# Group norm of layer 1 moved into the spectral transform, and the attention's weights multiplied out there

## The chip, the cores and the metric

The kernel runs on one core of a Trainium2 chip. The time is the device time of one execution in microseconds (us), and the figure of a kernel is the median of its runs. The granted clock of TensorE is a second number of each run: it has two levels, 1.2 and 2.4 GHz, shown as 0.50 and 1.00.

## The reference

The input is x of shape (4, 32, 128, 128) in float32: four batches of 32 images of 128 rows by 128 channels. Layers follow one another; each adds its result to x. Layer 0 is a graph attention and a state-space scan, layers 2 and 3 are attention, experts and a recurrence; none of them is touched. Layer 1 computes

```python
x = x + codano(gn(x))        # gn: 32 groups of 4 channels, over the 32 images of a batch
...
tokens = gn(x).reshape(128, 1, 128, 128)
tokens_norm = instance_norm(tokens)            # mean and variance of each image
k = fno_layer(tokens_norm, key_w, ..., (64, 64)); q = fno_layer(..., query_w, ...)
v = fno_layer(tokens_norm, value_w, ..., (128, 128))          # 16 heads from one channel
dprod = softmax(q . k over the 64*64 pixels)   # tokens of one batch against each other
attn = fno_layer(dprod @ v, proj_w, ...); attn = instance_norm(attn + tokens)
m = mixer(attn); out = instance_norm(m) + attn
```

where `fno_layer` is a product of low Fourier modes with weights plus a 1x1 skip path. Since a head differs from another by weights only, the products of query and key reduce to a Gram matrix of the 64x64 transforms of all tokens (skip paths) and to a few low modes (spectral weights).

## The kernel before, in words

All blocks run one after the other; between two blocks every engine meets at a barrier. Inside a block each engine has its own program, written out in order, and waits on semaphores (`wait_ge`); `Chain` makes each VectorE or GpSimd step wait for the one before it. All transfers go out on SyncE, in program order.

`group_norm` (L96) takes x one batch (2 MB) at a time into two buffers. ScalarE squares it (L130), TensorE sums columns by a matrix of ones (L140, L144), VectorE reduces to groups (L163), GpSimd takes the power -0.5 (L155) and VectorE normalises 128x4096 values twice (L176, L177) into `hg`, 8 MB in SBUF. SyncE waits for each load to land before it issues the next.

`token_spectra` (L1358) loads its tables, stores `hg` to the DRAM tensor `tokens` with one transfer (L1402), and then

- transforms rows: TensorE multiplies each image by a table of 65 columns (L1426), four images (a unit) per PSUM bank, and ScalarE copies them into `o1` (L1467), four banks in turn;
- takes statistics of every image on VectorE (L1497), has them totalled by two matmuls (L1431, L1432), and derives the instance norm's scale (L1508 to L1518), with one power on GpSimd (L1417);
- transforms columns (L1437 to L1442) into `z`, which ScalarE copies (L1474 to L1479); computes the low modes `xh` (L1448, L1450), which ScalarE scales (L1483); and sums the Gram matrix over 65 column blocks (L1457, L1458), scales it by a diagonal matmul (L1461) and stores it (L1404).

`token_attention` (L1557) loads the query and key weights and biases by 58 small transfers (L1622 to L1634), multiplies them out on VectorE into `da`, `db`, `row`, `r0` and `coef` (L1727 to L1772), meanwhile transposes the low modes on TensorE (L1667, L1668), and only then copies the transposed modes (L1776) and forms the heads' operands (L1784 on), scores, softmax and probabilities `pt`.

`attended_spectrum` (L1833) loads value and projection weights by 24 small transfers (L1871 to L1886), multiplies them into `w` on VectorE (L1923 to L1939), stores it to DRAM (`mode_weights`, L1890), and reads it back once per head, broadcast to all partitions (L1895); VectorE multiplies `xh` by it for 16 heads (L1947 to L1955) and TensorE mixes (L1981).

`graph_attention` (L181, layer 0) is not changed, but has in its prologue the group norm that the change uses: 16 chunks of eight images, each 512 KB, loaded on their own (L266), squared on ScalarE (L491), summed by a 128x32 matrix of ones in four column groups of the array, two for values and two for squares (L374), a reduction (L573), a matmul to group sums (L358), small VectorE and GpSimd steps, and two matmuls (L363, L364) that spread scale and shift over channels.

Of the kernel before, what the change touches and what calls it, by code (L numbers as in the profile page):

```python
# [13 lines left out]
f32 = mybir.dt.float32  # L14
# [6 lines left out]
P = 128  # L21
# [72 lines left out]


def group_norm(nc, src, hg, tag, G=32, eps=1e-5):  # L96

    J = C // G
    N = T * W * J
    with ExitStack() as ctx:  # L100
        s = Scope(nc, ctx, tag)
        xb = s.sb("xb", [P, 2, T * C])
        sq = s.sb("sq", [P, T * C])
        ones = s.sb("ones", [P, P])
        sums = s.sb("sums", [P, 2, G])
        var = s.sb("var", [P, G])
        rstd = s.sb("rstd", [P, G])
        half = s.sb("half", [P, G])
        ps = [s.ps(f"ps{j}") for j in range(2)]
        loaded, squared, summed, var_done, rstd_done, normed, ready = (  # L110
            s.sem(n) for n in ("loaded", "squared", "summed", "var_done", "rstd_done", "normed", "ready"))
        dch = s.sem("dch")
        block = ctx.enter_context(nc.Block())

        @block.sync
        def _(sp):
            for b in range(B):
                if b >= 2:
                    sp.wait_ge(normed, b - 1)
                sp.dma_start(xb[:, b % 2, :].rearrange("w (t c) -> w t c", t=T),  # L120
                             src[b].rearrange("t w c -> w t c")).then_inc(loaded, 16)
                sp.wait_ge(loaded, 16 * b + 16)

        @block.scalar
        def _(act):
            for b in range(B):
                act.wait_ge(loaded, 16 * b + 16)
                if b >= 1:
                    act.wait_ge(summed, b)
                act.activation(sq[:, :], xb[:, b % 2, :], ACT.Square).then_inc(squared, 1)  # L130

        @block.tensor
        def _(pe):
            pe.wait_ge(ready, 1)
            for b in range(B):
                pe.wait_ge(loaded, 16 * b + 16)
                if b >= 1:
                    pe.wait_ge(var_done, b)
                for j in range(8):
                    pe.matmul(ps[0][:, :], ones[:, :], xb[:, b % 2, 512 * j:512 * j + 512],  # L140
                              start=(j == 0), stop=(j == 7))
# [1178 lines left out]
SR = 64  # L1320
# [3076 lines left out]
```

## Time and profile before

| | us |
|---|---|
| median of 3 runs | 4502.13 (4489.3 to 4511.93) |
| the profiled execution | 4496.7 |
| its span | 4495.0 |
| TensorE matmul busy | 3571.1 (79%) |
| VectorE busy | 3190.4 (71%) |
| ScalarE busy | 2643.9 (59%) |
| GpSimd busy | 2526.4 (56%) |
| mean granted TensorE clock | 0.852 |

The durations in this text are from the profiled execution, whose own time is 1.7 us more than its span. A time such as 2518.35 is counted from the span's start. Busy shares are averages over all layers; for one block the windows and the timelines are read. In the rows PE is TensorE, PEld its weight loads, DVE VectorE, ACT ScalarE, POOL GpSimd, SP or SPq SyncE. A float32 matmul appears as two records (passes).

### The profile page before, as it was taken

The numbers are of one execution on the slowest core, as the hardware profiler recorded it, in microseconds if no ns is written. First come the engines' busy times: TensorE is split into PE (matmuls) and PEld (weight loads), VectorE is DVE, ScalarE is ACT, GpSimd is POOL, SyncE is SP. The second block draws the span as 40 slices with busy tenths as digits, with TensorE's granted clock in tenths as the row PEclk, the third lists the DMA queues.
The fourth block names the chain that finished last, engine by engine and source line by source line (L and its number), as shares of the span: only waits on it lengthen the run. The fifth ranks groups of instructions, "written<-read, shape, count | busy, mean of one in ns | idle before, by whom it ended". The sixth has DMA issues, their size and how long they took to land. (4 is left out here: it accounts for less than half of the span.)

```text
span 4495.0 us, 83074 instructions
## 1 busy us (share of the span) xinstructions
PE 3571.1 (79%) x29188; PEld 2331.2 (52%) x29188; DVE 3190.4 (71%) x6169; ACT 2643.9 (59%) x5155; POOL 2526.4 (56%) x2910
## 2 busy tenths in 40 slices
PE   7996599999999999999999676547884885658767
PEld 4764255555555555555555365315663652346636
DVE  4996388888888888888888342526994856159854
ACT  6885477778777778777787120004774627138553
POOL 4997678787787887787875210004785413012650
PEclk9998699999999999999999865676776977779678
DMA  3001000000000000000000230241222114760233
GB/s 83 25 25 48 7 4 20 20 11 20 20 20 20 16 15 20 20 20 20 11 18 23 72 85 2 81 167 57 76 62 70 52 52 115 251 167 1 62 90 108
DMA packets 376049, 231.29 MB, mean 51 GB/s; under 512 B 44288, under 2 KB 350920, under 8 KB 373576
## 3 DMA queue, kind: packets, MB, share of 16 engines
q1 hardware_dynamic: 375640, 225.98, 17.6%
q8 instruction: 239, 3.92, 0.4%
q14 instruction: 170, 1.39, 0.1%
HBM read 150.15 MB, written 75.76 MB: 50 GB/s over the span
## 5 line engine op out<-in xcount | busy, mean ns | idle before, releaser
L1222 DVE TENSOR_TENSOR_SCAN mam_hs<-mam_dA,mam_ps_b 128x1024 f32<-128x1024 f32 x512 | 1156.4, 2275 | 2.3 <-PE mam_ps_b L1027 2.1
L1041 PEld LDWEIGHTS mam_ps_h<-mam_ident,mam_hs 128*128 128x128 f32 x4096 | 460.4, 146 | 426.4 <-issue 422.6
L1027 PE MATMUL mam_ps_b<-mam_DB,mam_dtxt 32*128 32x512 f32 x2048 | 589.6, 651 | 85.6 <-DVE mam_hs L1222 82.8
L1160 ACT ACTIVATE mam_dA<-mam_dt,mam_A 128x496 f32<-128x496 f32 x1024 | 649.3, 703 | 0.7
L1168 ACT COPY mam_hTb<-mam_ps_h 128x512 f32<-128x512 f32 x768 | 424.9, 583 | 324.2 <-PE mam_ps_h L1041 320.3
L1041 PE MATMUL mam_ps_h<-mam_ident,mam_hs 128*128 128x128 f32 x4096 | 585.2, 288 | 27.7 <-ACT mam_hTb L1168 26.5
L825 POOL TENSOR_SCALAR mam_tap<-mam_xcp,mam_cw 128x512 f32<-128x512 f32 x192 | 300.7, 1566 | 18.7
L1232 DVE COPY mam_hTb<-mam_ps_h 128x512 f32<-128x512 f32 x256 | 175.9, 687 | 179.0 <-PE mam_ps_h L1041 179.0
L1053 PE MATMUL mam_ps_y<-mam_hTb,mam_WC 128*32 128x128 f32 x8192 | 281.3, 278 | 0.4 <-issue 0.4
L1053 PEld LDWEIGHTS mam_ps_y<-mam_hTb,mam_WC 128*32 128x32 f32 x8192 | 212.3, 111 | 122.6 <-issue 93.2
L1027 PEld LDWEIGHTS mam_ps_b<-mam_DB,mam_dtxt 32*128 32x128 f32 x2048 | 158.1, 186 | 221.6 <-issue 220.0
L826 POOL TENSOR_TENSOR mam_xs<-mam_xs,mam_tap 128x512 f32<-128x512 f32 x192 | 244.0, 1271 | 16.0
L855 POOL TENSOR_TENSOR mam_WC<-mam_cp,mam_m 128x128 f32<-128x128 f32 x512 | 220.4, 463 | 5.9 <-PE mam_ps_y L1053 5.7
L524 ACT ACTIVATE gat_ex<-gat_ps_s,gat_neg 128x128 f32<-128x128 f32 x512 | 154.5, 436 | 50.6 <-DVE gat_neg L607 50.6
L2227 POOL TENSOR_TENSOR l1t_rs<-l1t_va,l1t_half 128x8 f32<-128x8 f32 x64 | 108.1, 1689 | 126.0 <-DVE l1t_va L2547 125.8
L823 POOL TENSOR_SCALAR mam_xs<-mam_xcp,mam_cw 128x512 f32<-128x512 f32 x64 | 100.4, 1568 | 121.8 <-ACT mam_xcp L1113 121.4
L847 POOL TENSOR_TENSOR mam_DB<-mam_bt,mam_m 128x512 f32<-128x512 f32 x128 | 147.5, 1153 | 6.9 <-PE mam_ps_b L1027 6.5
L320 POOL TENSOR_TENSOR gat_ex<-gat_ex,gat_den 128x512 f32<-128x512 f32 x128 | 132.9, 1049 | 28.3 <-DVE gat_den L616 28.3
L966 PE MATMUL mam_ps<-mam_xs,mam_wdt 128*128 128x512 f32 x256 | 126.6, 618 | 5.3 <-issue 2.8
L831 POOL TENSOR_SCALAR mam_po<-mam_e 128x512 f32<-128x512 f32 x64 | 52.2, 816 | 137.8 <-ACT mam_e L1136 134.9
L3666 POOL MEMSET sma_half<- 128x4 f32 x1 | 0.1, 101 | 198.7 <-POOLq L81 198.7
L836 POOL TENSOR_TENSOR mam_dt<-mam_dt,mam_ln 128x512 f32<-128x512 f32 x64 | 81.7, 1277 | 47.9 <-DVE mam_ln L1260 47.9
(693 smaller groups left out, 8640.0 us busy)
## 6 DMA issues: line engine op xcount, KB each, us to landing
moe_wg<-in_L_ffn_weight SPq DMA_DIRECT2D x32, 1024.0 KB, 8.0
rnn_xr<-x SPq DMA_DIRECT2D x23, 512.0 KB, 5.4
l1y_wh<-mode_weights SPq DMA_DIRECT2D x16, 544.0 KB, 3.7
gat_hg<-in_x SPq DMA_DIRECT2D x16, 512.0 KB, 7.2
h<-gat_out SPq DMA_DIRECT2D x32, 256.0 KB, 2.3
mam_ht<-h SPq DMA_DIRECT2D x128, 64.0 KB, 2.0
mam_hr<-h SPq DMA_DIRECT2D x128, 64.0 KB, 2.0
mam_xt<-in_x SPq DMA_DIRECT2D x128, 64.0 KB, 2.0
```

What stands on the lines that cost most here:

```text
L524: last = act.activation(ex[:, i % 2, h, r, :], ps_s[h][:, r * W:(r + 1) * W], ACT.Exp, bias=neg[:, i % 2, h, r:r + 1])
L825: step(pool.tensor_scalar(tap[:, :, :], xcp[:, h, :, k:k + T], cw[:, h, k:k + 1], None, ALU.mult))
L826: step(pool.tensor_tensor(acc, acc, tap[:, :, :], ALU.add))
L847: pool.tensor_tensor(DB[:, g, :, :], bt[:, i % 2, g, :].unsqueeze(2).broadcast_to([P, S, T]), m32[:, :].unsqueeze(1).broadcast_to([P, S, T ...
L855: last = pool.tensor_tensor(WC[:, j, g, :, :], cp[:, i % 2, j, g, :].unsqueeze(2).broadcast_to([P, S4, T]), m32[:, :].unsqueeze(1).broadca ...
L1027: last = pe.matmul(ps_b[w % 2][:, n, :], steps[r, g * P:(g + 1) * P], DB[r, g, :, :].rearrange("p s t -> p (s t)"), start=True, stop=True, ...
L1041: last = pe.transpose(ps_h[n][:, q * P:(q + 1) * P], hs[:, w % 3, c:c + P], ident[:, :])
L1053: last = pe.matmul(ps_y[j * T:(j + 1) * T, g * P:(g + 1) * P], WC[:, j, g, q, :], hTb[:, gg % 2, j, q, :], start=(q == 0), stop=(q == S4 - 1),
L1160: act.activation(dA[:, h, :, n, 1:], dt[:, i % 2, h, :].rearrange("p (q t) -> p q t", q=Q)[:, :, 1:], ACT.Exp, scale=A[:, h, n:n + 1]).the ...
L1168: act.copy(hTb[:, gg % 2, j, :, :], ps_h[n][:, :].rearrange("p (q d) -> p q d", q=S4)).then_inc(hB_ready if n else hA_ready, 1)
L1222: dve.tensor_tensor_scan(hs[:, w % 3, :], dA[:, h, first:first + 2, :, :].rearrange("p q s t -> p (q s t)"), ps_b[w % 2][:, :, :].rearrang ...
L1232: dve.tensor_copy(hTb[:, gg % 2, 2 * (w % 2) + 1, :, :], ps_h[1][:, :].rearrange("p (q d) -> p q d", q=S4)).then_inc(hB_ready, 1)
```

## The change

The block `group_norm` is gone. `token_spectra` takes x itself. It loads x as 16 chunks of eight images into `hg` without waiting, sums them as graph attention's prologue does, and transforms the raw images' rows at once. ScalarE, which copies a unit's row transform out, now scales it by its channel's factor (`colsc`), for which it waits for the batch's norm (`norm_ready`); a channel's shift touches only the mode of row frequency 0, and VectorE adds it there (`constant_modes`). TensorE's order interleaves, for each batch, eight units with the four sums of the batch behind, and then the two group matmuls of that batch. VectorE makes the normalised tokens in three buffers of eight images (`normed`), from which the statistics are taken and which SyncE stores chunk by chunk (`save`).

The 58 and 24 small weight loads stand on SyncE between those stores, and the weights' products on VectorE behind the statistics. The totals of the instance norm come after the Gram matmuls on TensorE; `xh` is copied unscaled and scaled once at the end on VectorE. The two blocks behind lose these loads and products, and take the results from SBUF and DRAM. The tile `spec` is allocated after this block in place of before it.

```diff
+            for j in range(NC):
+                b, t0 = divmod(j * CH, T)
+                sp.dma_start(hg[:, j * CH:(j + 1) * CH, :], x1[b, t0:t0 + CH].rearrange("t w c -> w t c")
+                             ).then_inc(xin[j], 16)
...
+            def save(j):
+                sp.wait_ge(hn_ready, j + 1)
+                sp.dma_start(tok[j * CH:(j + 1) * CH].rearrange("n r c -> r n c"), hn[:, j % HB, :, :]
+                             ).then_inc(saved[j % HB], 16)
...
+            save(0)
...
+            for j, (name, ta, tb, tr) in enumerate((("query_w", qa, qb, qr), ("key_w", ka, kb, kr))):
+                src = wts[name][0].rearrange("h y x a -> y x h a")
+                for y in range(LKY):
+                    sp.dma_start(ta[y * L:(y + 1) * L, :, :], src[y, 1:LKX]).then_inc(w_loaded, 16)
+                    n += 1
+                save(2 + 2 * j)
+                sp.dma_start(tb[0:HF, :, :], src[0:HF, 0]).then_inc(w_loaded, 16)
+                sp.dma_start(tr[0:1, :, :], src[0:1, 0]).then_inc(w_loaded, 16)
...
+                save(3 + 2 * j)
...
+            assert n == WLOADS, (n, WLOADS)
+            for j in range(7, NC):
+                save(j)
+            sp.wait_ge(w_ready, 1)
+            sp.dma_start(wd.rearrange("h y a x -> y h a x"), mw[:, :, :, :]).then_inc(w_out, 16)
             sp.wait_ge(g_ready, 1)
             sp.dma_start(gram_d, gs[:, :]).then_inc(stored, 16)
             sp.wait_ge(stored, 16)
-            sp.wait_ge(saved, 16)
+            sp.wait_ge(w_out, 16)
+            for j in range(HB):
+                sp.wait_ge(saved[j], 16 * len(range(j, NC, HB)))
 
         @block.gpsimd
         def _(pool):
...
+            def sums(j):
+                pe.wait_ge(xin[j], 16)
+                pe.wait_ge(squared, j + 1)
+                b = j // CB
+                if j % CB == 0 and b >= 2:
+                    pe.wait_ge(red_ready, b - 1)
+                v, v2 = chunk(j), sq[:, j % 2, :]
+                for q, src in enumerate((v[:, 0:512], v[:, 512:1024], v2[:, 0:512], v2[:, 512:1024])):
+                    last = pe.matmul(ps_x[b % 2][32 * q:32 * q + 32, :], ones[:, :], src, start=(j % CB == 0),
+                                     stop=(j % CB == CB - 1), tile_position=(0, 32 * q))
+                last.then_inc(sums_done, 1)
+
+            def groups(b):
+                pe.wait_ge(red_ready, b + 1)
+                pe.matmul(ps_s[0:G, 4 * b:4 * b + 4], red[:, :], sel[:, :], start=True, stop=True).then_inc(grouped, 1)
+
+            def channels(b):
+                pe.wait_ge(wide_ready, b + 1)
+                pe.matmul(ps_s[:, 64 + 4 * b:68 + 4 * b], ext[:, :], gr[:, b, :], start=True, stop=True)
+                pe.matmul(ps_g[:, 0:2 * C], onesr[:, :], wide2[:, :, :].rearrange("p a c -> p (a c)"),
+                          start=True, stop=True).then_inc(spread, 1)
+
...
             pe.wait_ge(made, 1)
-            pe.wait_ge(summed, 1)
-            pe.matmul(ps_s[:, 0:4], su[:, :], mean_w[:, :], start=True, stop=True)
-            pe.matmul(ps_s[:, 4:8], sv[:, :], square_w[:, :], start=True, stop=True).then_inc(totalled, 1)
+            for j in range(CB):
+                sums(j)
+            pe.wait_ge(loaded, 80)
+            UB = UNITS // B
+            for b in range(B):
+                for i in range(CB):
+                    row_modes(UB * b + 2 * i)
+                    if b == 0 and i == 0:
+                        groups(0)
+                    if b < B - 1:
+                        sums(CB * (b + 1) + i)
+                    row_modes(UB * b + 2 * i + 1)
+                    if b == 0 and i == 0:
+                        channels(0)
+                if b < B - 1:
+                    groups(b + 1)
+                    channels(b + 1)
             pe.wait_ge(copied, UNITS)
...
+            pe.wait_ge(summed, 1)
+            pe.matmul(ps_s[:, 128:132], su[:, :], mean_w[:, :], start=True, stop=True)
+            pe.matmul(ps_s[:, 132:136], sv2[:, :], square_w[:, :], start=True, stop=True).then_inc(totalled, 1)
             pe.wait_ge(g_read, 1)
             pe.wait_ge(d_ready, 1)
-            pe.matmul(ps_s[:, 128:256], g0[:, :], diag[:, :], start=True, stop=True).then_inc(d_done, 1)
+            pe.matmul(ps_s[:, 256:384], g0[:, :], diag[:, :], start=True, stop=True).then_inc(d_done, 1)
 
...
+            def squares(j):
+                act.wait_ge(xin[j], 16)
+                if j >= 2:
+                    act.wait_ge(sums_done, j - 1)
+                act.activation(sq[:, j % 2, :], chunk(j), ACT.Square).then_inc(squared, 1)
+
+            def row_modes(u):
+                b = u * R // T
                 act.wait_ge(done, u + 1)
-                act.copy(o1[:, :, u * R:(u + 1) * R], ps[u % 4][:, 0:R * KA].rearrange("p (r k) -> p k r", r=R)
-                         ).then_inc(copied, 1)
+                act.wait_ge(norm_ready, b + 1)
+                act.activation(o1[:, :, u * R:(u + 1) * R], ps[u % 4][:, 0:R * KA].rearrange("p (r k) -> p k r", r=R),
+                               ACT.Identity, scale=colsc[:, b, 0:1]).then_inc(copied, 1)
+
...
+            def group_norm_of(b):
+                dve.wait_ge(sums_done, CB * (b + 1))
+                if b >= 1:
+                    dve.wait_ge(grouped, b)
+                step(dve.tensor_reduce(red[:, :], ps_x[b % 2][:, :].rearrange("p (t g j) -> p g t j", g=G, j=J), AX.XY,
+                                       ALU.add))
+                dve.sem_inc(red_ready, 1)
...
+                step.mark(dve.tensor_copy(rowsc[:, b, :, :], ps_g[:, 0:2 * C].rearrange("p (a c) -> p a c", a=2)))
+                step.join()
+                dve.sem_inc(norm_ready, 1)
+
...
+            def normed(j):
+                b, dst = j // CB, hn[:, j % HB, :, :]
+                if j >= HB:
+                    dve.wait_ge(saved[j % HB], 16 * (j // HB))
+                every = [P, CH, C]
+                step(TT(dst, hg[:, j * CH:(j + 1) * CH, :], rowsc[:, b, 0, :].unsqueeze(1).broadcast_to(every), ALU.mult))
+                step(TT(dst, dst, rowsc[:, b, 1, :].unsqueeze(1).broadcast_to(every), ALU.add))
+                dve.sem_inc(hn_ready, 1)
+                for n in range(CH):
+                    step.mark(dve.bn_stats(st[:, j * CH + n, :], hn[:, j % HB, n, :]))
+                step.join()
+
+            def constant_modes(b):
+                dve.wait_ge(copied, UNITS // B * (b + 1))
+                TS(o1[:, 0, batch(b)], o1[:, 0, batch(b)], colsc[:, b, 1:2], None, ALU.add).then_inc(k_fixed, 1)
+
+            group_norm_of(0)
+            for j in range(NC):
+                normed(j)
+                if j in (2, 5, 8):
+                    group_norm_of(j // 3 + 1)
+                if j in (5, 8, 10, 11):
+                    constant_modes((5, 8, 10, 11).index(j))
...
-        with nc.sbuf_tensor("hg1", [P, BT, C], f32) as hg:
-            group_norm(nc, x1, hg, "gn1")
-            token_spectra(nc, hg, wts["norm1_g"], wts["norm1_b"], tabs, xh, gram, tok, nrm)
...
-            dve.wait_ge(loaded, 16 * LOADS)
-            dve.wait_ge(prepared, 1)
+            dve.wait_ge(w_loaded, 16 * WLOADS)
+            dve.wait_ge(zeroed, 2)
...
+            step.mark(TT(sv[:, :, 0, 1], sv[:, :, 0, 1], rv[:, :, 1], ALU.subtract))
+            step.mark(TT(mw[:, :, 0, :], pr, vs.broadcast_to(full), ALU.mult))
...
+            dve.wait_ge(loaded, 80)
+            dve.wait_ge(totalled, 1)
+            step(dve.tensor_copy(mv[:, :], ps_s[:, 128:136].rearrange("p (a b) -> p a b", a=2)[:, :, 0]))
...
+            step.mark(TS(diag[:, :], ident[:, :], nrm[:, 0:1], None, ALU.mult))
+            step.join()
+            dve.sem_inc(nrm_ready, 1)
+            dve.sem_inc(d_ready, 1)
+            dve.wait_ge(x_read, NB)
+            step(TS(xh[:, :, :, :], xh[:, :, :, :], nrm[:, 0:1], None, ALU.mult))
+            step(dve.tensor_copy(xh[:, 0, 0, 0:1], gb[:, 1:2]))
...
-            dve.wait_ge(loaded, 16 * NL)
```

The lines that follow `dve.wait_ge(w_loaded, ...)` in the new `token_spectra` are the old ones of L1727 to L1772 and L1923 to L1939, moved; likewise the loads. Their names differ (`mw` for `w`, `sk`, `pskip`).

## Rows read from the trace of the kernel before

**Rows 1.** Windows: length; busy (count) of PE, PEld, DVE, ACT, POOL; PE clock; DMA.

```profile
2518.30:2620.60 102.30, 61.65 (x128) 26.15 (x128) 42.09 (x24) 14.47 (x4) 21.98 (x6) 0.80 0.30 82
2620.60:2680.80 60.20, 55.47 (x260) 55.47 (x261) 26.53 (x133) 12.04 (x32) 0.66 (x5) 0.50 0.51 143
2680.80:2753.40 72.60, 68.26 (x295) 56.74 (x295) 1.80 (x11) 12.65 (x25) 0.56 (x1) 0.62 0.01 1
...
2844.20:2872.90 28.70, 0.00 (x0) 0.00 (x0) 4.28 (x19) 0.00 (x0) 2.68 (x5) 0.50 0.21 39
```

**Rows 2.** Timeline of SyncE, group norm: start, us, line, transfer.

```profile
2518.35 61.40 SPq L120 DMA_DIRECT2D gn_xb<-x  x4
```

**Rows 3.** Timeline of TensorE, token spectra, key rows.

```profile
2625.33 54.87 PE L1426 MATMUL l1f_ps<-l1f_rows,hg 128*128 128x65 f32 x256 [22.42 <-DMA l1f_gb<-in_L_conv_norm_b]
2680.00 0.53 PE L1431 MATMUL l1f_ps_s<-l1f_mean_w,l1f_su 128*128 128x4 f32 x2
...
2680.82 15.55 PE L1437 MATMUL l1f_ps<-l1f_o,l1f_cols 128*65 128x512 f32 x34
...
2747.47 0.79 PE L1458 MATMUL l1f_ps_g<-l1f_zp 64*128 64x128 f32 x2
2748.62 0.80 PE L1461 MATMUL l1f_ps_s<-l1f_diag,l1f_g 128*128 128x128 f32 x2 [0.35 <-ACT l1f_g L1487]
```

**Rows 4.** Timeline of VectorE, token spectra, first and last of the chain.

```profile
2681.10 0.16 DVE L1508 COPY l1f_mv<-l1f_ps_s 128x2 f32<-128x2 f32 x1 [33.80 <-PE l1f_ps_s L1432]
...
2683.18 0.28 DVE L1518 TENSOR_SCALAR l1f_diag<-l1f_ident,nrm 128x128 f32<-128x128 f32 x1
```

**Rows 5.** Windows: graph attention's start, and the column transform L1437.

```profile
44.70:48.40 3.70, 2.77 (x6) 1.18 (x6) 0.00 (x0) 0.78 (x1) 1.26 (x1) 0.50 0.01 2
...
2684.00:2696.90 12.90, 12.90 (x36) 4.39 (x34) 0.00 (x0) 9.02 (x16) 0.00 (x0) 1.00 0.00 0
```

**Rows 6.** Graph attention's prologue: timelines of SyncE, ScalarE, TensorE; tile ps_s.

```profile
0.81 4.22 SPq L266 DMA_DIRECT2D gat_hg<-in_x  x4
...
10.17 21.00 SPq L266 DMA_DIRECT2D gat_hg<-in_x  x12
...
10.64 1.06 ACT L491 ACTIVATE gat_sq<-gat_hg 128x1024 f32<-128x1024 f32 x1 [0.77 <-DMA gat_hg<-in_x]
...
18.48 1.07 PE L374 MATMUL gat_ps_s<-gat_hg,gat_ones 128*32 128x512 f32 x2 [5.58 <-ACT gat_sq L491]
...
19.31 1.09 PE L374 MATMUL gat_ps_s<-gat_hg,gat_ones 128*32 128x512 f32 x2
...
L374 PE MATMUL gat_ps_s<-gat_hg,gat_ones x64: 589/617/1063, 6.4 to 38.5; 128*32 128x512 f32 x64
...
40.00 0.22 PE L358 MATMUL gat_ps_p<-gat_sel,gat_red 128*32 128x4 f32 x2 [0.87 <-DVEq L575]
...
42.70 1.20 PE L364 MATMUL gat_ps_p<-gat_wide,gat_onesr 32*128 32x256 f32 x2
```

**Rows 7.** VectorE: a 128x1024 operation (timeline) and the statistics (tile st).

```profile
2786.99 1.23 DVE L1784 TENSOR_TENSOR l1s_va<-l1s_xa,l1s_da 128x1024 f32<-128x1024 f32 x1
...
L1497 DVE BATCH_NORM_STATS2 l1f_st<-hg x128: 274/282/294, 2620.7 to 2645.2; 128x6 f32<-128x128 f32 x128
```

**Rows 8.** Head attention's start: timelines of SyncE, TensorE, VectorE.

```profile
2775.09 5.01 SPq L1634 DMA_DIRECT2D l1s_kr<-in_L_conv_key_w  x8
...
2757.44 0.42 PE L1668 MATMUL l1s_ps_p<-l1s_ident,l1s_xlob 128*128 128x128 f32 x1
...
2786.08 0.42 DVE L1776 COPY l1s_xa<-l1s_ps_p 128x256 f32<-128x256 f32 x1
```

**Rows 9.** Spectrum block's start: timelines of SyncE and VectorE.

```profile
2857.91 1.81 SPq L1886 DMA_DIRECT2D l1y_pb<-in_L_conv_proj_skip_b  x1
...
2868.56 11.30 SPq L1895 DMA_DIRECT2D l1y_wh<-mode_weights  x6
...
2872.86 1.29 DVE L1952 TENSOR_TENSOR l1y_t<-xh,l1y_wh 128x1088 f32<-128x1088 f32 x1 [6.00 <-DMA l1y_wh<-mode_weights]
```

More of the change, by code:

```diff
@@ L1393, in token_spectra, with chunk, batch @@
         NZU = len(parts) + 1
+        WLOADS = 6 + 2 * (LKY + 2) + 2 * (LKY // 2) + 3 + LKY + 5
+        def chunk(j):
+            return hg[:, j * CH:(j + 1) * CH, :].rearrange("p t c -> p (t c)")
+        def batch(b):
+            return slice(b * T, (b + 1) * T)
         @block.sync
         def _(sp):
-            for dst, src in ((rows[:, :], tabs["rows_all"]), (cols[:, :], tabs["gram_cols"]),
-                             (tcols[:, :, :].rearrange("p a k -> p (a k)"), tabs["tok_cols"])):
-                sp.dma_start(dst, src).then_inc(loaded, 16)
@@ L1443, in _ @@
                       ).then_inc(z_done, 1)
+            pe.wait_ge(red_ready, B)
             for n, ky in enumerate(ROWS):
@@ new lines, in _ @@
+            step.mark(TT(row[:, :], skips[0:1, 1, :], kb[0:1, :, 0], ALU.add))
+            step.mark(TS(r0[:, :], r0[:, :], unit, None, ALU.mult))
+            step.join()
+            for q, k, d, a, c, m in sides:
+                step.mark(TT(d[:, 0, :], a, k[:, :, 0], ALU.mult))
+                step.mark(TT(a, a, k[:, :, 1], ALU.mult))
+            step.mark(TT(row[:, :], row[:, :], skips[0:1, 4, :], ALU.mult))
+            step.join()
+            for q, k, d, a, c, m in sides:
+                step.mark(TT(d[:, 0, :], d[:, 0, :], c, ALU.add))
@@ new lines, in _ @@
+            step.mark(TS(row[:, :], row[:, :], unit, None, ALU.mult))
+            step.join()
+            for q, k, d, a, c, m in sides:
+                step.mark(TT(c, skips[0:m, 1, :], q[:, :, 0], ALU.mult))
+            step.join()
+            for q, k, d, a, c, m in sides:
+                step.mark(TT(d[:, 0, :], d[:, 0, :], c, ALU.add))
+            step.join()
+            for q, k, d, a, c, m in sides:
+                step.mark(TT(c, skips[0:m, 1, :], k[:, :, 0], ALU.add))
+            step.join()
@@ new lines, in _ @@
+            for q, k, d, a, c, m in sides:
+                step.mark(TT(c, c, q[:, :, 1], ALU.mult))
+            step.join()
+            for q, k, d, a, c, m in sides:
+                step.mark(TT(d[:, 1, :], c, a, ALU.subtract))
+            step.join()
+            for q, k, d, a, c, m in sides:
+                step.mark(TS(d[:, 0:2, :], d[:, 0:2, :], 2.0 * unit if d is da else two[:, 0:1], None, ALU.mult))
+            step.join()
+            for q, k, d, a, c, m in sides:
+                step.mark(TS(d[:, 2, :], d[:, 1, :], -1.0, None, ALU.mult))
@@ L1568, in token_attention @@
     HQ = NH // NQ
-    low = [n for n in range(NKY) if -LKY // 2 <= ROWS[n] < LKY // 2]
-    unit = float(SR * SR) / math.sqrt(SR * SR)
+    da, db, row, r0, coef = (mix_w[n] for n in ("da", "db", "row", "r0", "coef"))
     with ExitStack() as ctx:
```

455 lines of the change are left out of this document (192 added, 263 removed).

## Prediction

> **What bounds the kernel now.** I read the page's forty slices first: TensorE is at nine tenths or more in most of the first 22, where layer 0 runs, and layer 0 is untouched. The change is confined to the first three blocks of layer 1, so the next view is a table of windows over them [rows 1]. The reader is to see stretches of one kind from 2518.3 to 2872.9, 354.6 us together, in which no engine is full from end to end. In the group norm (102.3 us) TensorE works 61.7 us and waits for loads: its four loads of 2 MB go out one behind the other over 61.4 us [rows 2], since there are two buffers. In the next 60.2 us TensorE is busy for 55.5 us at a granted clock of 0.50, and VectorE, done early, idles. The 72.6 us after it are TensorE's too. For the head attention (2753.4 to 2844.2, 90.8 us) and the spectrum block behind it the timelines of single engines say more. The attention begins with weight loads: SyncE issues until 2780.1 and VectorE's first use of the attention's transposed operand comes at 2786.08, though TensorE had it at 2757.9 [rows 8]. The spectrum block runs 28.7 us with TensorE idle while SyncE loads value and projection weights, writes their product and reads it back [rows 1, 9].
>
> So each block is a serial chain: load, sums, normalise, row transform (L1426), column transform, Gram matrix; load weights, multiply; load weights, multiply, store, reload. What is worth asking is which chain ends last after the rearrangement.
>
> **Part one: group norm inside the transform.** Removed: the whole of [rows 1]'s first line, and the five table loads and barrier behind it. Moved: the 256 matmul records of L1426 (54.87 us for 32 units of four images, 1.71 us a unit [rows 3]) now run on raw images. Added: 16 sums of eight images, 4 group round trips, 16 normalise-and-statistics steps on VectorE, 16 stores in place of one. All times below count from the first load's issue, which was 2518.35 [rows 2] and does not move.
>
> Loads. Graph attention already loads 16 such chunks: 12 take 21.00 us of issue, 1.75 us each, and chunk 3 is used at 10.64, 9.8 us after the first issue at 0.81 [rows 6]. Here five table loads stand between chunks 1 and 2; eight such loads cost 5.1 us there (5.07 to 10.17), so I add 3.2 us: chunk 3 is squared at 13.0, which takes 1.06.
>
> Sums. In graph attention four products share the array by column groups, and each is two passes. A pass takes up to 1.06 us, and the second set starts 0.83 us behind the first (18.48, 19.31) [rows 6], so a chunk costs 2 x 0.83, about 1.7 us. Its bounds are 1.06 (passes wholly overlapped) and 2.1 (end to end); with 12 of them between batch 0 and batch 3 that is 8 us less or 5 more. The shortest passes take 0.59 [rows 6], at the high clock; there I take half, 0.85. Batch 0 is summed by 14.1 + 1.7 = 16.
>
> The clock is the open cost. With high clock a unit of L1426 would cost 0.85 us. The trace shows L1426 alone held at 0.50 for its whole length [rows 1], and a stretch of graph attention in which TensorE was busy 2.77 of 3.70 us, 512-column matmuls among it, still at 0.50; it was at 1.00 in the unbroken run of 512-column matmuls of L1437 [rows 5]. The new mixture has 1.7 us of sums to 3.4 us of L1426 (two units). I take the low clock, as L1426 is two thirds of it.
>
> The Trainium skill's page "TensorE: Matmul & The Clock Gate", section "What's actually happening", says otherwise in its plain form: the engine is throttled by default and sustained activity releases it. By that rule TensorE, busy without a break here, would run at the full clock, which is the second case below; the rule is contradicted by L1426 in this trace, which was busy without a break at 0.50.
>
> The sum at the low clock, per batch: 8 units x 1.71 = 13.65, 4 sums x 1.7 = 6.8, together 20.45 us. VectorE's side of a batch is less: a chunk is two 128x1024 operations (1.23 us [rows 7]) and eight statistics (128 in 24.8 us, 0.194 each [rows 7]), with the gaps of a chain 4.17 us; three chunks, 12.5 us, precede the next round trip. A round trip stops TensorE from the group matmul at 40.00 to the end of the spread at 43.90, 3.9 us [rows 6]. Steps: 16.0; first unit, group matmul, sum 4, second unit and spread, 23.2; six units and three sums, 38.5; round trip, 42.4; batch 1 and round trip, 66.8; batch 2 and round trip, 91.1; batch 3 has no sums, 104.8; copy and the correction of the constant modes, 105.6. VectorE's last four chunks (17 us), the statistics' totals (2 us) and the weight products (busy 4.28 us in the last stretch of [rows 1], with their gaps some 5, and as much again for the attention's) lie beside the column transform and the Gram matmuls: those take from 2680.82 to 2748.26, 67.4 us [rows 3], and are unchanged. So they cost nothing; without that cover they would cost 29 us.
>
> New at the end: the totals come after the Gram matmuls. TensorE's totals to VectorE's first read 1.1 us (2680.00 to 2681.10), VectorE and GpSimd to the diagonal 2.4 us (to 2683.46) [rows 3, 4]; this used to be hidden. From the diagonal matmul to the next block is 4.8 us as before (2748.62 to 2753.4) [rows 1, 3]. The scaling of the 1088-column spectrum on VectorE (1.29 us for that width [rows 9]) lies beside this matmul and the store. Sum: 105.6 + 67.4 + 1.1 + 2.4 + 4.8 = 181.3 us, where it was 2753.4 - 2518.35 = 235.1. Gain 53.8.
>
> Stores and small loads. 82 small loads are now queued on SyncE between stores 0 and 7. They took 26.7 us (2753.4 to 2780.1) and 15.5 us (2844.2 to 2859.7) [rows 8, 9], 42 us or 0.51 each. After the chunk loads, at 31, they end near 77 with the seven stores between. VectorE's chunk 10 needs store 7 landed, and begins at about 96 in this case. Slack about 15 us; the cost is nothing until a load takes 0.7 us.
>
> **Part two: head attention.** Weight loads and the weight products leave. What remains before the copy L1776 is GpSimd's preparation and four transposes, ended at 2757.86 [rows 8]; GpSimd loses six short instructions before them. The copy moves from 2786.08 to about 2757.6. Gain 28.5 (bounds 28.2 and 29.2). Next in line is VectorE's own product chain, so nothing new waits.
>
> **Part three: spectrum block.** SyncE can issue the first head's weights at the block's start. From that issue at 2868.56 to VectorE's use at 2872.86 took 4.3 us [rows 9]; so 2848.5 and a gain of 24.4. The memsets that remain end before that.
>
> Total 53.8 + 28.5 + 24.4 = 106.7 us. The profiled execution took 4496.7 us (span 4495.0 and 1.7 around it), which gives 4390. The median of the three runs is 5.4 us higher and they spread by 23; I stay with the profiled one.
>
> **Rivals.** (a) The sums lift the clock. Then TensorE needs 10.2 us a batch and VectorE sets the pace: from 23.8, twelve chunks x 4.17 = 50.0, three round trips of 0.7 + 4.6 = 16, correction: 90. That is 15.6 us less, 4374. For it: the shortest passes of these sums in graph attention are 0.59 [rows 6], so bursts of them do get the high clock there. Against: each round trip idles TensorE, and L1426 dominates. (b) SyncE's queue falls behind partly: loads behind bulk transfers cost more, as the last of the 24 did, 1.81 us [rows 9], or the eight behind chunk loads, 0.64 each [rows 6]. At 1.0 us a load VectorE is held 40 - 15 = 25 us: 4415; at 1.4 us 4448. (c) Slower than before, by the same place at a higher price: at SyncE, VectorE waits for a store slot behind the 82 loads. The gain of 106.7 is used up when they take (42 + 15 + 107)/82 = 2.0 us each; at 3.0 us it is 82 more: 4579. The longest single load in the rows took 1.81, and 24 together 15.5, so this is remote. (d) The change moves work but the chain in blocks two and three was set by something else, so that only part one pays: 4443. The timelines speak against it, since VectorE's wait ends with the last load.
>
> **How the numbers follow.** Forecast 0.62; (a) 0.21; (b) 0.10; (d) 0.03; (c) 0.02; no difference 0.02. The unknowns: clock (down 16), VectorE's chunk (slack of 8 us a batch, so nothing), SyncE (up 25), the phase in which the clock rises and falls in the column transform (3 us either way), run-to-run (11 us either way). The forecast's own range is 4378 to 4402; with (a) and the near end of (b) 4358 to 4420. About 0.5%, 22 us, is what a measurement of this kernel tells from no change; all of the forecast, (a), nearly all of (b) and (d) lie beyond it: faster 0.95, same 0.03, slower 0.02.
>
> **What would show it.** The stage from first load to the attention's first store setup at 181 us; the raw row matmuls at 1.7 us a unit and PE clock 0.5 between 16 and 105; column transform starting 105 us in; VectorE idle several us per batch ahead of the reduction; the head attention 62 us instead of 90.8; the spectrum block's first product 4.3 us in. A column transform starting near 90 is (a); VectorE waiting on a token store is (b) or (c). Wrong if the Gram matmuls end and VectorE still has weight products to do.

## The result, and the profile after

The changed kernel took 4394.97 us, the median of 3 runs (4393.14 to 4400.9), against 4502.13; the ratio is 0.977, interval 0.975 to 0.979. The profiled execution took 4393.14 (span 4391.3). The forecast of 4390 is 5 us off; against the profiled execution, from whose counterpart before it was worked out, it is 3.

Layer 0, unchanged, lets layer 1 begin at other times from one execution to the next (last section), so all times below count from the first load's issue, here 2517.66 (SPq L1362). First the stages, as in [rows 1]; columns are span and length, busy time (count) of each engine, granted clock, DMA share, GB/s:

```profile
2522.70:2527.10 4.40, 3.62 (x16) 0.59 (x16) 0.00 (x0) 2.11 (x2) 0.00 (x0) 0.60 1.05 288
2527.10:2535.00 7.90, 7.16 (x54) 4.02 (x54) 2.60 (x11) 2.40 (x3) 0.56 (x1) 1.00 1.15 347
2535.00:2536.60 1.60, 0.06 (x1) 0.00 (x0) 1.57 (x2) 1.60 (x4) 0.00 (x0) 0.95 1.15 346
2536.60:2622.10 85.50, 78.36 (x339) 56.17 (x340) 55.05 (x154) 23.55 (x40) 1.63 (x3) 0.50 0.43 111
2622.10:2689.40 67.30, 67.30 (x292) 56.06 (x292) 26.07 (x100) 11.49 (x23) 0.00 (x0) 0.63 0.11 33
2700.00:2761.70 61.70, 37.84 (x129) 29.56 (x129) 34.47 (x56) 2.97 (x5) 3.83 (x10) 0.53 0.00 1
2761.70:2765.90 4.20, 0.00 (x0) 0.00 (x0) 0.00 (x0) 0.00 (x0) 2.28 (x3) 0.50 0.70 209
```

The first five lines show the new block without its head (the first load to the first sum) and its tail (the totals to the next block). With both it took 182.3 us (2517.66 to 2700.00), where the first three lines of [rows 1] took 235.1. The head attention has 61.7 us for 90.8, and the 28.7 us ahead of the spectrum block's first product are 4.2. TensorE's timeline shows one period of the raw transform (two units and a sum), a round trip, the last Gram matmul, the totals and the diagonal:

```profile
2564.47 3.68 PE L1492 MATMUL l1f_ps<-l1f_rows,l1f_hg 128*128 128x65 f32 x16
2568.07 1.07 PE L1474 MATMUL l1f_ps_x<-l1f_hg,l1f_ones 128*32 128x512 f32 x2
2568.93 1.07 PE L1474 MATMUL l1f_ps_x<-l1f_hg,l1f_ones 128*32 128x512 f32 x2
2569.94 3.68 PE L1492 MATMUL l1f_ps<-l1f_rows,l1f_hg 128*128 128x65 f32 x16
...
2577.31 0.27 PE L1480 MATMUL l1f_ps_s<-l1f_sel,l1f_red 128*32 128x4 f32 x2
2579.61 0.58 PE L1484 MATMUL l1f_ps_s<-l1f_gr,l1f_ext 32*128 32x4 f32 x2 [2.02 <-DVEq L1623]
2580.06 1.20 PE L1485 MATMUL l1f_ps_g<-l1f_wide,l1f_onesr 32*128 32x256 f32 x2
2581.18 1.12 PE L1492 MATMUL l1f_ps<-l1f_rows,l1f_hg 128*128 128x65 f32 x4
...
2688.71 0.79 PE L1541 MATMUL l1f_ps_g<-l1f_zp 64*128 64x128 f32 x2
2689.44 0.59 PE L1543 MATMUL l1f_ps_s<-l1f_mean_w,l1f_su 128*128 128x4 f32 x2
2693.26 0.77 PE L1547 MATMUL l1f_ps_s<-l1f_diag,l1f_g 128*128 128x128 f32 x2 [2.81 <-DVEq L1749]
```

VectorE's timeline: the last reduce, ahead of which it idled, the totals, for which it waited 40.6 us after the weight products, and its first use in each of the two blocks behind:

```profile
2601.57 0.69 DVE L1608 TENSOR_REDUCE l1f_red<-l1f_ps_x 128x32 f32<-128x512 f32 x1 [6.59 <-issue]
2690.59 0.16 DVE L1736 COPY l1f_mv<-l1f_ps_s 128x2 f32<-128x2 f32 x1 [40.60 <-PE l1f_ps_s L1544]
2703.77 0.42 DVE L1915 COPY l1s_xa<-l1s_ps_p 128x256 f32<-128x256 f32 x1 [2.83 <-PE l1s_ps_p L1860]
2765.93 1.29 DVE L2026 TENSOR_TENSOR l1y_t<-xh,l1y_wh 128x1088 f32<-128x1088 f32 x1 [6.11 <-DMA l1y_wh<-mode_weights]
```

From the first load to the spectrum block's first product it was 354.5 us (2518.35 to 2872.86 [rows 2, 9]) and is 248.3: 106.2 gained, where 106.7 had been worked out. The span is 103.7 us shorter, so the rest of it is 106.2 + 0.7 (first load earlier) - 103.7 = 3.2 us longer, in blocks that are the same.

### The profile page after: what moved, and what is told of

Read it like the earlier page. It is cut to its first block and busy times, and to the rows that moved or that the text cites. A ratio compares the mean times of both kernels' runs of the same rounds, so it can differ in the third digit from the quotient of the medians.

```text
span 4391.3 us, 83296 instructions
## 1 busy us (share of the span) xinstructions
PE 3545.1 (81%) x29212; PEld 2311.5 (53%) x29212; DVE 3199.4 (73%) x6223; ACT 2646.2 (60%) x5167; POOL 2506.2 (57%) x2915
```

## The experiments

"To the column transform" and "to the product" are from the first load's issue; "rest" is from the product to the end of the span. All are of the one profiled execution; medians are of all its runs.

| | first load at | to the column transform | to the product | rest | median | ratio to before (95%) |
|---|---|---|---|---|---|---|
| before | 2518.35 | 162.5 | 354.5 | 1622.1 | 4502.13 | |
| after | 2517.66 | 104.4 | 248.3 | 1625.4 | 4394.97 | 0.977 (0.975 to 0.979) |
| after_again | 2528.59 | 103.5 | 247.6 | 1615.1 | 4402.12 | 0.978 (0.976 to 0.980) |
| e1_norm_only | 2526.34 | 109.3 | 307.0 | 1626.8 | 4458.79 | 0.992 (0.989 to 0.994) |
| e2_weights_only | 2515.51 | 158.7 | 298.1 | 1617.1 | 4436.39 | 0.987 (0.984 to 0.989) |
| e3_sums_ahead | 2526.00 | 101.9 | 245.8 | 1621.1 | 4400.36 | 0.979 (0.977 to 0.981) |
| e4_totals_early | 2518.94 | 104.2 | 245.6 | 1626.8 | 4395.28 | 0.977 (0.975 to 0.980) |
| e5_dve_load | 2523.60 | 105.9 | 250.0 | 1619.5 | 4394.82, one run | |
| e6_loads_twice | 2523.85 | 133.1 | 278.1 | 1626.4 | 4430.0, one run | |
| e8_products_late | 2514.62 | 104.2 | 257.7 | 1625.8 | 4399.83, one run | |
| e7_sums_follow | 2527.57 | 83.2 | 227.5 | 1627.7 | 4379.75 | 0.973 (0.972 to 0.975) |
| e9_no_stop | 2529.68 | 65.4 | 216.1 | 1618.4 | 4372.36 | 0.971 (0.970 to 0.973) |
| e10_all | 2526.97 | 65.3 | 213.6 | 1620.1 | 4359.41 | 0.968 (0.966 to 0.970) |
| e11_best | 2527.42 | 61.0 | 200.6 | 1621.8 | 4358.4 | 0.970 (0.967 to 0.972) |

### The parts apart: e1_norm_only, e2_weights_only

In words, as both edits are long: e1 has the new `token_spectra` without the 82 loads and both products, and `token_attention` and `attended_spectrum` as in the kernel before. e2 has `group_norm` and `token_spectra` as in the kernel before, with the 82 loads behind the token store and both products behind the statistics.

> Part one alone: the group norm works inside the transform as in the changed kernel, and the weight loads and weight products of the head attention and of the spectrum block are back in their own blocks, as before. My account (three independent parts of 53, 29 and 24.4 us, as the two traces show them block by block): head attention 90.8 us again instead of 61.7, spectrum block 28.7 us to its first product instead of 4.3, so 4395 + 53.5 = about 4448 us, and the column transform still starts 104 us after the first load. Rival one (the weight loads cost the transform something between the token stores, or the weight products do on VectorE): the transform itself gets shorter by some us and the whole is 4440 or less. Rival two (part one pays only because the other two go with it): 4470 or more.

> Parts two and three alone: group norm in its own block as before, but all 82 small weight loads are issued in the transform behind the one large token store, and both weight products are made on VectorE beside the Gram matmuls. My account: 4502 - 53.5 = about 4449 us, the sum of the gains of the two single parts then equals that of the whole change (107 us). Rival one (the loads stand behind the 8 MB store and are late, over 1 us each): VectorE ends its products behind the Gram matmuls and the gain is 40 us or less. Rival two (the gains of the parts overlap): the two gains of this run and of the run with part one alone sum to clearly more than 107.

Both parts pay, and the gains add as far as the runs can tell. To the product e1 gained 47.5 us and e2 56.4, together 103.9 of 106.2; by the ratios 38 and 59 us (each known within 11), 97 together against 102 (after) and 100 (after_again) for the whole. In e2 the attention's first copy to the spectrum block's product took 66.0 us (2747.53 to 2813.56), for 119.4 before and 65.9 after: these two parts are 53.4, where the forecast had 28.5 + 24.4 = 52.9. e2 gained 3 us more in the unchanged group norm, whose loads took 57.4 us for 61.4. e1 fell 5 us short at the start of part one, and its median is 11 us over what was expected. TensorE's clock rose there and fell again within a stop of 0.7 us for ScalarE (2537.6), so that it had 2.8 us at 1.00 (1.43 busy) for 7.9 (7.16 busy) in the changed kernel. The 5.7 us of work that it did less at 1.00 take twice as long at 0.50, which makes the shortfall an estimated 5.7 us:

```profile
2534.80:2537.60 2.80, 1.43 (x12) 0.19 (x8) 0.00 (x0) 1.51 (x2) 0.00 (x0) 1.00 1.22 290
2538.30:2634.60 96.30, 89.45 (x384) 62.89 (x384) 58.71 (x163) 26.02 (x43) 2.18 (x4) 0.50 0.46 121
```

### What has slack: e5_dve_load, e6_loads_twice, e8_products_late

```diff
@@ e5, VectorE, each chunk
+                step(TS(spare[:, :, :], hg[:, j * CH:(j + 1) * CH, :], 2.0, None, ALU.mult))
@@ e6, SyncE, behind each of the 82 small loads
+                sp.dma_start(skips_[:, j, :], flat(name)).then_inc(w_twice, 16)
@@ e8, VectorE: both products
-            dve.wait_ge(w_loaded, 16 * WLOADS)   ... ahead of the totals
             step(dve.tensor_copy(xh[:, 0, 0, 0:1], gb[:, 1:2]))
+            dve.wait_ge(w_loaded, 16 * WLOADS)   ... behind the scaling of xh
```

> The changed kernel with one more 128x1024 operation on VectorE in each of the 16 chunks (into a tile that nobody reads), 1.26 us a chunk. My account (TensorE sets the pace in the raw row transform, VectorE idles 6.6 us ahead of each later reduce and 2.1 us ahead of the first): the three chunks before the first round trip add 3.8 us to 2.1 us of slack, so the column transform starts 1.7 us later, at about 106 us after the first load's issue instead of 104.4, and the rest is hidden under column transform and Gram matmuls. Rival (VectorE sets the pace): 12 chunks by 1.26 us, the column transform starts 15 us later, at 119.5.

> The changed kernel with each of its 82 small weight loads issued a second time, right behind the first, into tiles that nobody reads. SyncE then issues some 50 us longer ahead of its later token stores. My account (the store slots have about 15 us of slack at the 0.5 to 0.6 us that a load takes, and VectorE waits beyond it): VectorE waits for store slots in chunks 7 to 10, the column transform starts 34 us later (138 us after the first load instead of 104), all of it is lost at the end. Rival (SyncE's queue never matters, since stores have slots to spare or small loads are cheap in number): column transform at 104 to 108 us, no change.

> The changed kernel with both weight products moved on VectorE from ahead of the layer norm's totals (beside the Gram matmuls) to behind its scaling of the spectrum, where nothing long covers them. My account (they are hidden only by the Gram matmuls): 9.2 us of products and the store of the mode weights now end the block, 5 us of it beside the diagonal matmul and the store of the Gram matrix, so the head attention starts 7 us later, 189 us after the first load instead of 182.4. Rival (the block's tail of 4.8 us or an earlier wait covers them too): less than 2 us.

e5: 105.9 us to the column transform, 1.5 more for 20 us of added VectorE work, and 119.5 if VectorE had set the pace. So TensorE sets it. e6: 28.7 us later, 29.8 at the product, all kept at the end (4430). VectorE's waits in e6, by what ended them, name the store slots (total, times, longest):

```profile
DVE l1f_hn L1656 <- DMA tokens<-l1f_hn: 44.4, 6, 11.2
```

The last small load was issued 120.6 us after the first chunk's (2644.48), for 77.5 in the changed kernel: 43.1 us more queue cost 28.7, so 14.4 were slack, where 15 had been worked out. Rival (b)'s place is real, and at one load each it costs nothing: the changed kernel has no row of this kind. e8: the attention's first transpose comes 194.0 us after the first load (2708.65) instead of 185.0 (2702.62). Uncovered the products cost 9.1 us, not the 7 expected. SyncE's program has the store of the mode weights ahead of that of the Gram matrix: the Gram result was ready at 2691.32 and was stored at 2699.69, so the tail did not run beside the products but behind them.

### The diagonal: e4_totals_early

```diff
+            pe.wait_ge(summed, 1)
+            pe.matmul(ps_s[:, 128:132], su[:, :], mean_w[:, :], start=True, stop=True)
+            pe.matmul(ps_s[:, 132:136], sv2[:, :], square_w[:, :], start=True, stop=True).then_inc(totalled, 1)
             pe.wait_ge(z_read, NZU)
             pe.wait_ge(z_fixed, 1)
```

> The changed kernel with the two matmuls of the layer norm's totals moved from behind the Gram matmuls to before them. My account: VectorE's and GpSimd's chain to the diagonal then lies beside the Gram matmuls, the diagonal matmul comes 1.6 us after the last Gram matmul instead of 4.6, and the time is 3 us lower, about 4392. Rival (the chain is hidden by the copy of the Gram matrix and something else sets the end): no change, and the diagonal still comes 4 us or more after the Gram matmuls. The two differ by less than the runs spread, so the trace decides.

```profile
2690.66 0.79 PE L1544 MATMUL l1f_ps_g<-l1f_zp 64*128 64x128 f32 x2
2691.81 0.80 PE L1547 MATMUL l1f_ps_s<-l1f_diag,l1f_g 128*128 128x128 f32 x2 [0.36 <-ACT l1f_g L1590]
```

The diagonal comes 1.15 us after the last Gram matmul's start, for 4.55 in the changed kernel (2688.71 to 2693.26), and so the block ends 3.4 us sooner behind that start. The totals' matmuls now lie ahead of it, so to the product it is 2.7 us; the medians can't tell that.

### The clock: e3_sums_ahead, e7_sums_follow, e9_no_stop

```diff
@@ e3, TensorE: a sum behind each of a batch's first four units
+                    if b < B - 1 and i < CB:
                         sums(CB * (b + 1) + i)
@@ e7, TensorE: the sums as the chunks land; VectorE: norms behind chunks 0, 1, 2
+            for u in range(UNITS):
+                row_modes(u)
+                if u < NC - CB:
+                    sums(CB + u)
+                if u in (5, 10, 15):
+                    groups(u // 5)
@@ e9, against e7
-                if u in (5, 10, 15):
+                if u in (5, 10, 18):
```

e9 also has the spread of the last batch behind unit 23 in place of 18, and the constant-mode corrections behind chunks 3, 4, 4 and 5 in place of 4, 6, 8 and 9.

> The changed kernel with another order on TensorE: the four sums of a batch go one behind each of the first four units of the batch before (instead of one behind every second unit), the group matmul behind the fifth unit and the spread behind the seventh, so that none of the three round trips of 3.9 us stops the row transforms. ScalarE's squares move with them. Theory A (the stops, the first one of 1.6 us at 2535 among them, hold the clock down): the granted clock stays at 1.00 as it was from 2527 to 2535, VectorE sets the pace with 12 chunks of 4.3 us and 3 group norms of 4.6 us, the column transform starts some 83 us after the first load, and the time is about 4374. Theory B (the 65-column row matmuls keep the clock at 0.50 whether there are stops or not): only the three round trips go, 11.7 us, the transform starts 93 us after the first load, about 4384. If neither, VectorE's chain takes the place of the trips and nothing is gained: 4395.

> The changed kernel with all 16 sums made as the chunks land, one behind each of the first 12 units of the row transform, the three later group norms on VectorE right behind its first three chunks, the group matmuls behind units 6, 11 and 16 and the spreads behind units 7, 13 and 18, and the constant-mode corrections behind chunks 4, 6, 8 and 9. Nothing should stop TensorE between its first unit and the column transform. Theory A (the clock stays at 1.00 once it has risen and nothing stops TensorE for several us, as it was from 9.5 us after the first load until a stop): units and sums take 0.85 us each, VectorE's correction behind chunk 9 sets the start of the column transform at 73 us after the first load instead of 104, and the time is about 4364. Theory B (at 0.50 whatever TensorE does after the first loads are in): 12 sums of 1.86 and 28 units of 1.71 us follow one another, the column transform starts at 93 us, 4384. Theory C (the high clock holds as long as sums are among the matmuls and falls with the row matmuls alone): 16 units at high, 20 at low, column transform at 70 to 80 us.

> The kernel in which the sums follow the loads, with the third group matmul behind unit 19 and its spread behind unit 23 (there it stood 2.5 us behind unit 16, waiting for VectorE, and the high clock was gone behind it), and the constant-mode corrections behind chunks 3, 4, 4 and 5. Theory A (the high clock lasts as long as TensorE isn't stopped, whatever it multiplies): all 32 units at 0.85 us, VectorE's last correction sets the start of the column transform, about 65 us after the first load instead of 83, 4365 us. Theory C (row matmuls alone let the clock fall): from unit 13 on, where the sums end, within some units the clock is 0.50 with TensorE unbroken; 17 units at 1.71, column transform at about 72 us, 4370.

e3 gained little, and shows why. Windows: high clock, a stop in which TensorE waited 9.3 us for VectorE (three chunks stood ahead of the second reduce), and then 69 us without a stop:

```profile
2535.50:2548.40 12.90, 12.15 (x94) 6.43 (x94) 6.45 (x21) 7.14 (x10) 0.56 (x1) 1.00 1.15 347
2548.40:2557.70 9.30, 0.06 (x1) 0.00 (x0) 8.82 (x21) 0.48 (x1) 0.00 (x0) 0.68 0.85 250
2557.70:2626.80 69.10, 69.04 (x298) 52.05 (x298) 43.50 (x122) 19.96 (x34) 1.63 (x3) 0.50 0.36 87
```

The same kind of mixture runs at 1.00 before the stop and at 0.50 behind it, 69.04 of 69.10 us busy. So theory A and theory B are each half wrong: here the mixture kept a high clock and did not raise a low one. The three round trips of 3.9 us went and a stop of 9.3 came, which leaves about the 2.5 us gained. e7 has no stop until its last group matmul, which waited 2.5 us for VectorE (2571.1 to 2573.65). Its clock was 1.00 for 33 us and 0.50 from there on, but it fell 1 us ahead of that stop, while row matmuls ran without a break. Windows of e7, first the stretch up to the stop, then the fall in it, then behind the stop:

```profile
2537.10:2571.10 34.00, 33.50 (x258) 20.02 (x258) 17.58 (x52) 19.79 (x28) 1.64 (x3) 0.98 0.80 216
2569.50:2570.00 0.50, 0.50 (x7) 0.50 (x6) 0.47 (x2) 0.17 (x1) 0.00 (x0) 1.00 0.15 2
2570.00:2570.50 0.50, 0.50 (x6) 0.50 (x4) 0.50 (x1) 0.30 (x1) 0.00 (x0) 0.57 0.21 3
2570.50:2571.00 0.50, 0.50 (x3) 0.44 (x3) 0.50 (x1) 0.00 (x0) 0.00 (x0) 0.50 0.22 3
2573.70:2603.20 29.50, 29.49 (x134) 28.51 (x134) 23.93 (x63) 7.16 (x15) 0.54 (x1) 0.50 0.32 76
```

None of the theories' times for e7 came: the column transform began at 83.2 us. TensorE waited 7.6 us ahead of it for VectorE's last correction, so VectorE set this time at either clock, and A's 73 had its chain too short. e9 took the stop of 2.5 us away and e10, with the same order here, too. Windows of e9 and of e10 (two each):

```profile
2539.20:2580.40 41.20, 40.42 (x321) 26.54 (x320) 21.01 (x68) 23.62 (x36) 2.18 (x4) 1.00 0.71 191
2580.40:2594.00 13.60, 13.60 (x73) 13.44 (x72) 12.75 (x34) 3.82 (x8) 0.00 (x0) 0.58 0.36 80
```

```profile
2536.50:2569.00 32.50, 32.00 (x250) 18.68 (x251) 16.19 (x51) 19.32 (x27) 1.64 (x3) 1.00 0.83 225
2569.00:2586.00 17.00, 16.71 (x144) 16.01 (x143) 12.43 (x36) 8.12 (x17) 0.54 (x1) 1.00 0.27 64
```

In e9 the clock fell inside the last nine units (at 2582.6), with row matmuls alone and no stop; in e10 it held to the end. In e10 VectorE's last correction, for which TensorE waited 6.3 us, sets the start of the column transform (65.3 us), as theory A says. In e9 (65.4 us) that correction waited only 0.2 us for ScalarE's copy of the last unit, so VectorE and the slower row matmuls ended nearly together there. What decides between these two executions stays open.

### Putting it together: e10_all, after_again, e11_best

```diff
@@ e10, TensorE, among the Gram matmuls
+                if k == 40:
+                    pe.wait_ge(summed, 1)
+                    ... the two matmuls of the totals
@@ e11, VectorE, in the loop over chunks
-                    if j == (3, 4, 4, 5)[b]:
+                    if j == (3, 4, 4, 4)[b]:
                         constant_modes(b)
+                if j == 8:
+                    dve.wait_ge(z_read, 1)
+                    dve.memset(z[0:1, 0, :], 0.0).then_inc(z_fixed, 1)
```

> The same with the two matmuls of the layer norm's totals set among the Gram matmuls, ahead of the 41st of 65 modes, where VectorE has the statistics. Expected: 3.4 us less than without them behind the Gram matmuls, as where this alone was done, so 4361 to 4366 us. Rival: VectorE's last chunks now end later than the Gram matmuls allow (11 chunks of 4.3 us and 11 us of products behind the last correction) and TensorE waits inside the Gram matmuls, so that nothing or less is gained.

> The changed kernel itself once more, beside the others on the same chip, unchanged. All theories: 4395 us within 5, and the first load of layer 1 issued between 2515 and 2528 us, since that time differs by up to 13 us between profiled executions of kernels whose layer 0 is the same.

> The kernel with the sums behind the loads and the totals among the Gram matmuls, with two waits on VectorE taken away that the trace of that kernel shows: the clearing of the Gram operand's constant row stands behind chunk 8 instead of behind the statistics (6.6 us of wait ahead of the first Gram matmul), and the last constant-mode correction behind chunk 4 instead of chunk 5 (6.3 us of wait ahead of the column transform, of which 4.3 can go). Expected: column transform 61 us after the first load instead of 65, Gram matmuls without a wait, together 11 us less, about 4349. Rival (VectorE's remaining 11 chunks and the weight products, 60 us from the last correction, now end behind the Gram matmuls): the diagonal waits for VectorE and the gain is half of that or less, 4355 or more.

e10_all is faster than both kernels: 0.968 of before, and 4359.4 beside 4402.1 of the changed kernel on the same chip. Of these 43 us, 34 lie ahead of the product (213.6 for 247.6); the profiled executions differ by 31, as what lies outside varies. TensorE's waits in e10 show what is left, both ended by VectorE:

```profile
PE l1f_ps_g L1542 <- DVE l1f_z L1657: 6.6, 1, 6.6
PE l1f_ps L1517 <- DVE l1f_o L1640: 6.3, 1, 6.3
```

The first of them is the named rival in part: VectorE, late with its last chunks, held the Gram matmuls up, ahead of the first and not among them. To the product e10 is 2.5 us sooner than e9, for 3.4 expected; by the medians it is 13, more than this edit explains.

after_again came out as the first time, 247.6 us to the product. Its first load was issued at 2528.59, 0.6 us beyond the range named for it, and its median is 2 us beyond the 4395 within 5. e11's profiled execution took both waits away (1.9 us are left) and reached the product 13.0 us sooner, 11 of them as expected; the column transform ran at 1.00 (14.2 us) where e10's had 0.86 (16.4 us). Windows of e11, the end of the row matmuls, the stop of 1.95 us behind them and the column transform:

```profile
2569.00:2586.50 17.50, 17.21 (x149) 16.53 (x147) 12.92 (x36) 8.42 (x18) 0.54 (x1) 1.00 0.26 62
2586.50:2588.40 1.90, 0.01 (x1) 0.00 (x0) 1.86 (x11) 0.48 (x1) 0.00 (x0) 1.00 0.18 7
2588.40:2602.60 14.20, 14.14 (x35) 4.68 (x36) 13.52 (x32) 9.14 (x17) 0.00 (x0) 1.00 0.45 117
```

Its six runs spread from 4350.5 to 4388.4, wider than any other's, and the median is e10's, so that it is better is not shown.

## Why the prediction was right

Step by step, with the forecast first.

- Loads: chunk 3 squared from 13.0; it was 9.9 (2527.60). That is graph attention's 9.8 [rows 6] again, although the five table loads took 3.0 us of issue (2518.72 to 2521.67). Issue was not what the chunks waited for; adding it was wrong.
- Sums of batch 0 done at 16.0; VectorE reduced at 12.3. Two units, a sum and the spread behind it took 4.2 us for 7.2 (2529.80 to 2533.96), at a clock of 1.00, of which the forecast had nothing. A stop of 1.6 us followed: ScalarE's program has the copy of the first two units, which waits for the first norm, ahead of the next chunk's square. The next round trip began at 33.7 for 38.5, 4.8 us early.
- Sums among units 1.7 us each; the period of two units and a sum is 5.47 us (2564.47 to 2569.94), 3.60 for the pair and 1.87 for the sum. With 3.42 for two units alone, a sum costs 2.05, near the upper bound that was given (2.1). Behind another sum it costs 1.7 (0.85 from one set to the next, for passes of 1.07), so what the overlap saves is mostly lost at the change to and from row matmuls. A batch took 25.95 us for 24.35.
- Round trips 3.9 each: 2577.31 to 2581.18, 3.87. The last batch 13.65: 13.92.
- Column transform at 105.6: 104.4. The 4.8 us won by the end of batch 0 and the 3.6 us lost behind it (two batches at 1.6, the rest in the last units and the correction) all but cancelled. That they did is luck: the sum was better than its terms.
- Column transform to totals 67.4: 67.4. Totals 1.1: 1.15. Chain to the diagonal 2.4: 2.67. From the diagonal to the next block 4.8: 6.7; the Gram store went out 1.35 us behind the diagonal, as before, and the block ended 5.4 us behind that store for 3.5. A block ends with SyncE clearing its semaphores one by one: 23 of them before and 56 after, which would be 0.057 us each (an estimate from these two traces). e1, with 52, took 5.1, which fits; e2, with 27, took 4.2, 0.4 more than it would give. No run changed this alone, so it is not shown.
- Part two: 28.5 with the block at 62; measured 29.1 and 61.7. Part three: 24.4 with the first product 4.3 us in; 24.5 and 4.2. e1 and e2 show both apart from part one.
- Stores and small loads free, ending near 77 with 15 us of slack: they ended at 77.5, and e6 gives 14.4 us of slack.
- VectorE beside TensorE: a chunk 4.31 for 4.17. It idled 6.7 and 6.6 us ahead of the last two reduces, for 8, and 2.1 ahead of the one before them; e5 shows that TensorE set the pace.
- Cover of the products: 9.1 us without it (e8). That is a third of the 29 us named; the chunks and statistics that make up the rest were not uncovered.
- To the product 106.7 us gained: 106.2. That the median came within 5 us is luck in part too: the rest of the span, which the forecast left as it was, was 3.2 us longer, and it varies by 12.6 us over the executions of the table.

Rival (a), the sums lift the clock, was worked out at 90 us to the column transform and 4374. In this kernel it failed: the clock was 1.00 from 2527.1 to 2535 and 0.50 from 2536.6 on. The forecast's reason for the low clock was incomplete, though. It took the 65-column matmuls to hold it down, and a unit to cost 0.85 us at the high clock; measured are 0.93 (e10, four units, 2573.18 to 2576.90). e3, e7, e9, e10 and e11 show them, with and without sums, at 1.00 for up to 50 us, once the clock was up. So the low clock that the forecast rested on was right for this order of work, and not for these matmuls as such.

What ends the high clock stays open. In the changed kernel it fell in the stop of 1.6 us at 2535, and in all six executions with this stop (after, after_again, e4, e5, e6, e8) it fell in it or within 0.7 us behind it. In e1 it fell in a stop of 0.7 us, and in e3 3.3 us into the one of 9.3. But in e7 and e9 it fell in row matmuls without a break, in e7 1 us ahead of the next stop, in e9 6.9 us behind one of 0.3 us. A stop of 1.95 us in e11 left it at 1.00, and one of 2.1 us in the kernel before did too (2586.8 to 2588.9). So a stop is neither needed for a fall nor enough for one. That the stop right behind the rise ended the high clock in the changed kernel is likely, and not shown.

The Trainium skill's page "TensorE: Matmul & The Clock Gate", section "What's actually happening", has sustained activity release the clock. The 69 us of e3 at 0.50 speak against it in that plain form. By the same section an idle engine returns to the low clock. The fall inside the stop of 9.3 us in e3 agrees with that; the falls of e7 and e9, in which TensorE was never idle, it does not explain.

## What to carry to other kernels

Write a forecast for a moved chain as times from one event, and check single terms as well as the sum: here an early start of 4.8 us and 3.6 us of slower work hid each other. Where TensorE has just reached its high clock, look at what comes next: the same instructions in an order that keeps it fed (e7, e9) gave 21 and 32 us to the product, while taking three round trips out and leaving a stop of 9.3 us in (e3) gave 2. Read the clock in windows finer than the stop that is blamed: in e7 it had fallen before the stop began. Small loads are free up to the slack of what is queued behind them, and doubling them once on the chip shows where that ends.

## What the runs showed of the hardware

- The start of layer 1 lay between 2514.6 and 2529.7 us in 14 profiled executions, though layer 0 is the same. In two executions of the same kernel it was 2517.66 and 2528.59, and the span was 4391.3 both times. Stages compared by absolute times would have been wrong by up to 15 us; the rest behind the product varied from 1615.1 to 1627.7.
- A mixture of 65-column and 512-column matmuls ran at either clock for tens of us, 2.04 us for a unit and a sum at 1.00 (e7, 2557.76 to 2559.80) and 3.76 at 0.50 (e3, 2568.62 to 2572.38).
- A load that broadcasts 4 bytes to 128 partitions behind the strided one of `proj_w` held SyncE for 4.3 us (2548.65), ten times the others' 0.43. With each load doubled (e6) 5.9 us stood at the second strided load, so it is no cost of the broadcast. The second strided load passed only 1.1 us on to the next one, so why these loads hold the queue stays open.
